# Moving the split maxima, the stores and the gates to other steps of a hand-placed schedule (transformer block on one core)

## The chip, the cores and the metric

The kernel runs on one core of a Trainium2 chip (trn2). The metric is the device time of one execution in microseconds (us), the median of several. Of the kernel before there are three timed executions and one profiled one.

The engines are named as in the profile: PE is TensorE (matmuls; PEld is its weight load), DVE is VectorE, ACT is ScalarE, POOL is GpSimd, SPq is the queue of SyncE, which here issues every DMA. Each engine works through its own instructions in the order in which they are written. It waits only on semaphores.

## What is computed

One transformer block with adaptive layer norm, on x of 2 x 2048 tokens and 256 channels in float32. Cut to what matters:

```
mod = silu(c) @ wmod                      # shifts, scales, gates of both halves
h = layernorm(x) * (1 + ca) + sa
q, k, v = split(h @ W_qkv.T + b_qkv)      # 16 heads of 16
attn = softmax(where(causal, q @ k.T / 4, -inf))
x = x + ga * ((attn @ v) @ W_out.T + b_out)
h = layernorm(x) * (1 + cb) + sb
def mole(x, W, b, A, Bm, Rw):             # E = 3 experts of rank R = 8
    gates = softmax(x @ Rw)
    return x @ W + b + (1 / R) * sum_e(gates_e * (x @ A_e)) @ Bm_e
x = x + gb * mole(relu(mole(h, W1, ...)), W2, ...)
```

## The kernel before

**Steps.** The attention is cut into 32 *units*: one batch, one block J of 512 queries, one group g of 4 heads (`UNITS`). A unit has 4(J+1) *steps*, one for each tile of 128 keys, and there are 320 steps in all. `FIRST[u]` is the first step of unit u. Before step 0 lie 27 steps of preparation (`BEGIN` = -27), and after step 319 some 50 more, in which the last two blocks of the feed-forward half are done.

**One attention step.** PE makes the logits of two pairs of heads (`logits`, L636, and with a mask on the diagonal L641), ACT takes their exponentials (L845), and PE multiplies those by the values two steps later (L700). The last four steps of a unit are on the diagonal, where the widths shrink from 512 to 128.

**The maxima.** The softmax needs each query's maximum before the logits are exponentiated. So a unit's logits are first made once more in the other orientation: PE makes a *pair* (L663, in the diagonal with L671) into two of three PSUM banks, which are taken in turn (`M_BANKS` = 3), and DVE reduces them (`maximum`, L983). `pair_steps` spreads the pairs of unit u over the steps before that unit, about two a step. When the last is done, DVE takes the maximum over blocks and splits it into a rounded part and a rest (`make_parts`, L996, L999, L1000; these are the *split parts*). PE transposes them in step `FIRST[u] - 3` (`turn_maxima`, L682; I call this the *turn* of unit u), DVE copies the result (`copy_parts`, L1008), SP loads it as two more rows of the query tile (L544). PE's turn waits for `m_parts`, which the last instruction of `make_parts` raises.

**The products of the two linear halves.** A block is 256 tokens, and there are 16 of them. The chain `S_CHAIN` makes q, k and v of a block (`s_...`), and `F_CHAIN` does the output projection and the feed-forward half (`f_...`). Each element is a piece of work and its distance in steps from the piece ahead. `S_START` and `F_START` are the first steps of each block. `place()` lays them out, and a PE product gets a step of its own. What a product leaves in its PSUM bank is read by ACT, DVE or POOL at the head of the next step. The products take banks from the same three as the pairs.

**The order within a step** is written out in the loop of each engine. PE: first logits, the turn if there is one, half of the pairs, second logits, values, the other pairs, products. DVE: what products left, `copy_parts`, the step's maxima, then other pieces (statistics, gates), and `make_parts` last of all. SP: loads of queries and keys, `o_rows`, `load_maxima`, then the pieces.

**Pieces that the change touches.** `s_store` issues twelve DMAs of a block's q and k into DRAM (L567), two steps after `s_v`. `stored(b, c)` tells from which step on a block of queries or keys may be read back. `f_load` issues the loads of a block's attention output and row sums (two each, L588 and L589) and of its x (L596). `f_exp` and `f_exp2` are the exponentials of the gates on ACT, `f_gate` and `f_gate2` are what DVE does to them afterwards (L1101 to L1113: sum, reciprocal, scaling, product with the low-rank values and its split), and `f_zturn`, `f_zturn2` are the PE transposes of the result.

Of the kernel before, what the change touches and what calls it, by code (L numbers as in the profile page):

```python
# [15 lines left out]
NH, HD = 16, 16  # L16
# [45 lines left out]
S_CHAIN = [("s_load", 0), ("s_stat", 1), ("s_xhat", 1), ("s_turn", 1), ("s_qk0", 2), ("s_qk1", 1), ("s_v", 1),  # L62
           ("s_store", 2)]
D_CHAIN = [("d_load", 0), ("d_inv", 2), ("d_store", 1)]
F_CHAIN = [("f_load", 0), ("f_norm", 2), ("f_proj", 3), ("f_stat", 2), ("f_xhat", 1), ("f_turn", 1), ("f_base", 0),
           ("f_route", 2), ("f_exp", 1), ("f_gate", 1), ("f_zturn", 1), ("f_hid0", 1), ("f_hid1", 1), ("f_hid2", 1),
           ("f_hid3", 1), ("f_down0", 2), ("f_down1", 1), ("f_exp2", 1), ("f_gate2", 1), ("f_zturn2", 1),
           ("f_low", 1), ("f_out", 2)]
# [141 lines left out]
def key_loads():  # L210

    at = {s: [] for s in range(BEGIN - 1, END)}
    for kb, (u, c) in enumerate(K_BLOCKS):
        need = min(STEP_OF_PAIR[u, k] for k, pair in enumerate(PAIRS[u]) if pair[0] == c)
        step = max(need - LOAD_LEAD, keys_free(kb))
        b, J, _ = UNITS[u]
        assert WHEN["s_store", 2 * (NJ * b + c) + 1] < step < need, (kb, u, c, step, need)
        at[step].append(kb)
    return at
# [5 lines left out]
def query_loads():  # L225

    at = {s: [] for s in range(BEGIN - 1, END)}
    for u in range(NU):
        need = STEP_OF_PAIR[u, 0]
        step = max(need - LOAD_LEAD, FIRST[u - Q_BUFS + 1] if u >= Q_BUFS else BEGIN)  # L230
        b, J, _ = UNITS[u]
        assert WHEN["s_store", 2 * (NJ * b + J) + 1] < step < need, (u, step, need)
        at[step].append(u)
# [6 lines left out]
def build_program(nc, x, cT, wmod, wqkvT, bqkv, bv, woutT, bout, w1, b1, ar1, bl1, w2, b2, ar2, bl2, out):  # L240
# [5 lines left out]
    with ExitStack() as whole:  # L246
# [264 lines left out]
        with nc.Block() as block:  # L511
            @block.sync
            def _(sp):
# [43 lines left out]

                def s_store(n):
                    b, t0 = batch(n), n * TB % S
                    full, hi = s_buffer(n)  # L560
                    for w, (rows, lows) in enumerate(((q_rows, (0, 0, 1)), (k_rows, (0, 1, 0)))):
                        sp.wait_ge(qk_done, 2 * n + w + 1)
                        for slot, low in enumerate(lows):
                            for c in range(KC):
                                m = KC * w + c
                                src = full[:, m] if low else hi[:, m].bitcast(F32)
                                sp.dma_start(rows[b, 8 * c:8 * c + 8, slot * HD:(slot + 1) * HD, t0:t0 + TB],  # L567
                                             src).then_inc(qk_stored[min(n, EARLY)], 16)

# [7 lines left out]
                def d_store(c):  # L577
                    sp.wait_ge(d_done, c + 1)
                    sp.dma_start(r_rows[c].rearrange("h (k x) -> (h k) x", k=P // NH), den[:]).then_inc(d_stored, 16)

                def f_load(n):
                    c, cols = n // 2, slice(n % 2 * TB, n % 2 * TB + TB)
                    sp.wait_ge(d_stored, 16 * (c + 1))
# [3 lines left out]
                    for k in range(KC):  # L587
                        sp.dma_start(fo[:, k, :], o_rows[c, 8 * k:8 * k + 8, 0:HD, cols]).then_inc(fo_in, 16)  # L588
                        sp.dma_start(fd[:, k, :], r_rows[c, 8 * k:8 * k + 8, cols].unsqueeze(1)  # L589
                                     .broadcast_to((8, HD, TB))).then_inc(fo_in, 16)  # L590
                    if n == 0:
# [10 lines left out]
                pieces = {"s_load": s_load, "s_store": s_store, "d_load": d_load, "d_store": d_store,  # L602
                          "f_load": f_load, "f_out": f_out}
                sp.wait_ge(tables, 13)
# [355 lines left out]
            def _(dve):  # L960
# [185 lines left out]
                for s in range(BEGIN, END):  # L1146
# [151 lines left out]
```

## Time and profile before

| | before |
|---|---|
| timed executions | 1594.4, 1594.85, 1597.65 us |
| median | 1594.85 us |
| profiled execution | 1604.27 us, of which the span shown is 1602.5 us |
| PE busy | 1344.8 us, 84% of the span |
| DVE, ACT, POOL busy | 918.7, 790.3, 386.8 us |
| mean granted clock of PE | 0.843 of full speed |

A row of the waits names who waited, for whom, the sum in us, the number of times and the longest. A row of the timeline has the start and the duration in us, the engine, the line, the operation, what it writes and reads, and in brackets the idle time of the engine just ahead of it and what ended that. A row of the windows has a stretch, its length, the busy time of each engine with the number of instructions, the granted clock of PE (1.00 is 2.4 GHz, 0.50 is 1.2 GHz), the share of time in which the DMA engines were busy, and GB/s.

### The profile page before, as it was taken

What the parts mean: (1) busy time and instruction counts of PE and PEld (TensorE: products, weight loads), DVE (VectorE), ACT (ScalarE), POOL (GpSimd) and SP (SyncE); (2) the same over time, 40 slices, a digit from 0 to 9 for tenths busy, and PEclk for the clock granted to TensorE, in tenths of its full rate; (3) what the DMA queues carried; (4) which work ended last, traced back from release to release, by engine and by line L of the source; (5) the groups of instructions that cost most, each with busy time, mean ns of one, the idle gap of its engine ahead of it and who ended that gap; (6) DMA issues with size and microseconds to landing.
All of it is one profiled execution on the core that took longest, in us unless ns stands there. A gap on an engine that the chain in (4) does not pass through costs nothing. (4 is left out here: it accounts for less than half of the span.)

```text
span 1602.5 us, 26356 instructions
## 1 busy us (share of the span) xinstructions
PE 1344.8 (84%) x10096; PEld 770.6 (48%) x10096; DVE 918.7 (57%) x1886; ACT 790.3 (49%) x1193; POOL 386.8 (24%) x534
## 2 busy tenths in 40 slices
PE   4576787998898898889899998988999999999656
PEld 3553443454553555345444454545455465455246
DVE  6353576667666474745644656676667656662023
ACT  2423364566655454654345545555545555465421
POOL 4310112133223211221202122324233231321041
PEclk8758598899997896988859767999899797799857
DMA  5414142225312112231101332132212121100100
GB/s 160 137 56 120 47 121 77 62 57 165 97 51 63 48 28 67 86 103 40 51 21 55 102 97 73 35 103 67 84 58 58 33 61 48 43 17 15 35 20 14
DMA packets 85943, 107.22 MB, mean 67 GB/s; under 512 B 11306, under 2 KB 59378, under 8 KB 85820
## 3 DMA queue, kind: packets, MB, share of 16 engines
q1 hardware_dynamic: 85820, 105.54, 23.0%
q8 instruction: 82, 1.34, 0.4%
q14 instruction: 41, 0.34, 0.1%
HBM read 66.97 MB, written 38.01 MB: 66 GB/s over the span
## 5 line engine op out<-in xcount | busy, mean ns | idle before, releaser
L983 DVE TENSOR_REDUCE mx<-ps 128x1 f32<-128x512 f32 (+3 forms) x1152 | 707.6, 656 | 405.9 <-PE ps L663 211.2
L845 ACT ACTIVATE prob<-ps 128x1024 f32<-128x1024 f32 (+3 forms) x640 | 552.5, 902 | 419.9 <-PE ps L641 217.2
L663 PE MATMUL ps<-kst,qst 48*128 48x512 f32 (+3 forms) x1280 | 322.7, 500 | 120.1 <-DVE mx L983 91.6
L700 PE MATMUL ps<-prob,vw 128*17 128x512 f32 (+3 forms) x2560 | 341.0, 609 | 0.0
L663 PEld LDWEIGHTS ps<-kst,qst 48*128 48x128 f32 x1280 | 144.8, 212 | 401.8 <-issue 293.0
L636 PE MATMUL ps<-qst,kst 50*128 50x512 f32 (+3 forms) x1280 | 295.8, 456 | 7.7 <-ACT prob L845 6.8
L636 PEld LDWEIGHTS ps<-qst,kst 50*128 50x128 f32 x1280 | 138.5, 208 | 70.0 <-ACT prob L845 29.5
L509 POOL TENSOR_TENSOR hid_lo<-hidf,hid_hi 128x512 fp32r<-128x512 f32 x56 | 71.8, 1282 | 276.0 <-ACT hid_hi L934 276.0
L933 ACT ACTIVATE hidf<-ps 128x512 f32<-128x512 f32 x64 | 38.3, 598 | 112.1 <-PE ps L785 108.1
L671 PE MATMUL ps<-mask_q,pick 64*128 64x128 bf16 x1024 | 86.0, 250 | 0.0
L700 PEld LDWEIGHTS ps<-prob,vw 128*17 128x17 f32 x2560 | 43.9, 98 | 86.9 <-issue 54.9
L709 PE MATMUL ps<-fhT_hi,w_hi 128*128 128x256 f32 x256 | 83.9, 328 | 1.1 <-ACT zgT L922 0.9
L641 PE MATMUL ps<-mask_k,pick 64*128 64x128 bf16 x1024 | 83.0, 242 | 0.0
L794 PE MATMUL ps<-w_hi,hid_hi 128*128 128x284 f32 x256 | 73.2, 312 | 5.0 <-DVE hid_lo L509 4.4
L709 PE MATMUL ps<-fhT_lo,w_hi 128*128 128x256 f32 x256 | 76.8, 300 | 0.0
L709 PE MATMUL ps<-fhT_hi,w_lo 128*128 128x256 f32 x256 | 76.5, 299 | 0.0
L1201 POOL TENSOR_TENSOR sf<-sf,s_hi 128x512 f32<-128x512 f32 x28 | 36.9, 1318 | 149.5 <-ACT s_hi L898 149.5
L794 PE MATMUL ps<-w_lo,hid_hi 128*128 128x284 f32 x256 | 70.0, 300 | 0.0
L1121 DVE COPY fz<-ps 128x28 f32<-128x28 f32 x32 | 6.0, 188 | 103.7 <-PE ps L794 103.7
L709 PEld LDWEIGHTS ps<-fhT_hi,w_hi 128*128 128x128 f32 x256 | 53.5, 209 | 23.5 <-issue 12.0
L1243 POOL TENSOR_TENSOR fx<-fx,yg 128x256 f32<-128x256 f32 x32 | 23.5, 734 | 153.7 <-DVE yg L1122 153.7
L794 PEld LDWEIGHTS ps<-w_hi,hid_hi 128*128 128x128 f32 x256 | 50.1, 196 | 14.5 <-issue 9.1
(157 smaller groups left out, 1741.4 us busy)
## 6 DMA issues: line engine op xcount, KB each, us to landing
kst<-k_rows SPq DMA_DIRECT2D x160, 192.0 KB, 3.9
qst<-q_rows SPq DMA_DIRECT2D x64, 192.0 KB, 3.8
o_rows<-o_sb SPq DMA_DIRECT2D x32, 256.0 KB, 2.1
q_rows<-s_hi SPq DMA_DIRECT2D x56, 128.0 KB
k_rows<-s_hi SPq DMA_DIRECT2D x56, 128.0 KB
sx<-in_x SPq DMA_DIRECT2D x16, 256.0 KB, 5.4
fo<-o_rows SPq DMA_DIRECT2D x32, 128.0 KB
fd<-r_rows SPq DMA_DIRECT2D x32, 128.0 KB
```

Source lines behind the costliest of these rows:

```text
L509: eng.tensor_tensor(parts[1], src, parts[0].bitcast(F32), ALU.subtract).then_inc(ready, 1)
L636: last = pe.matmul(ps[:, banks[a], 0:width], kst[half, slot, p, t % 4 * P:(t % 4 + 1) * P], qst[half, u % Q_BUFS, p, skip:BLK], start=True ...
L641: last = pe.matmul(ps[:, banks[a], 0:P], pick[half, w - a + 1], mask_k[half, w - a + 1], start=False, stop=(w == 1))
L663: last = pe.matmul(ps[:, M_BANK + banks[a], at:at + width], qst[half, u % Q_BUFS, p, i * P:(i + 1) * P], kst[half, K_SLOT[u, c], p, 0:widt ...
L671: last = pe.matmul(ps[:, M_BANK + banks[a], at + width - P:at + width], pick[half, w - a + 1], mask_q[half, w - a + 1], start=False, stop= ...
L700: last = pe.matmul(ps[32 * h:32 * h + HD + 1, O_BANK, skip:BLK], vw[:, (NJ * b + t // 4) % V_BUFS, t % 4, g * GH + h, :], prob[:, s % P_BU ...
L709: last = pe.matmul(out, lhs(i, k), rhs(j, k), start=(k == 0 and n == 0), stop=(stop and k == chunks - 1 and n == len(PASSES) - 1))
L794: last = pe.matmul(ps[:, bank, 0:D + ZP], hid[i][:, m, t * P:(t + 1) * P], w2_p[j][:, m, :], start=(e == 0), stop=(e == len(DOWN) - 1))
L845: act.activation(prob[:, s % P_BUFS, 2 * p:2 * p + 2, 0:width], ps[:, bank:bank + 2, 0:width], ACT.Exp).then_inc(a_free, 1)
L933: act.activation(hidf[:].rearrange("p m t -> p (m t)"), ps[:, bank, :], ACT.Relu)
L983: dve.tensor_reduce(mx[:, u % 2, a, both, i, c], ps[:, M_BANK + bank, 0:n * width].rearrange("p (h x) -> p h x", h=n), AX, ALU.max).then_i ...
L1201: pool.tensor_tensor(full[:, half], full[:, half], hi[:, half].bitcast(F32), ALU.subtract).then_inc(qk_done, 1)
```

## The change

Three things are done to the tables and the loops, and no arithmetic is changed.

1. `make_parts(u)` is called in step `PARTS_STEP[u]`: `FIRST[u] - 4` for the first eight units, as before, and `FIRST[u] - 5` for the other 24. The pairs of a unit must be done by then, so that those of units from the ninth on have a last step one earlier. The turn stays in step `FIRST[u] - 3`.
2. `s_store` becomes four pieces of three DMAs each, in the step of `s_v` and the three after it. The last group is thus issued one step later than all twelve were, and `stored` follows it.
3. In the feed-forward chain `f_load` is cut in two: the loads of the second half of the channels and of x form `f_rest`, a step later, and `f_norm` still follows two steps after that. `f_gate` and `f_gate2` come two steps after their exponentials where it was one. A block's chain is so up to three steps longer, and where blocks queue up, later ones start up to three steps later.

```diff
 S_CHAIN = [..., ("s_v", 1),
-           ("s_store", 2)]
+           ("s_store0", 0), ("s_store1", 1), ("s_store2", 1), ("s_store3", 1)]
-F_CHAIN = [("f_load", 0), ("f_norm", 2), ... ("f_exp", 1), ("f_gate", 1), ... ("f_gate2", 1), ...]
+F_CHAIN = [("f_load", 0), ("f_rest", 1), ("f_norm", 2), ... ("f_exp", 1), ("f_gate", 2), ... ("f_gate2", 2), ...]
...
-    return WHEN["s_store", 2 * (NJ * b + c) + 1] + LOAD_LEAD + 1
+    return WHEN["s_store3", 2 * (NJ * b + c) + 1] + LOAD_LEAD + 1
+
+
+PARTS_STEP = [FIRST[u] - MAX_LEAD - (1 if u < 2 * NG else 2) for u in range(NU)]
+PARTS_AT = {s: u for u, s in enumerate(PARTS_STEP)}
...
-            todo.append((max(free), FIRST[u] - MAX_LEAD, u, k))
+            todo.append((max(free), PARTS_STEP[u] + 1, u, k))
...
-                def s_store(n):
+                def s_store(n, m):
...
+                    w, c = divmod(m, KC)
+                    rows, lows = ((q_rows, (0, 0, 1)), (k_rows, (0, 1, 0)))[w]
+                    sp.wait_ge(qk_done, 2 * n + w + 1)
+                    for slot, low in enumerate(lows):
+                        src = full[:, m] if low else hi[:, m].bitcast(F32)
+                        sp.dma_start(rows[...], src).then_inc(qk_stored[min(n, EARLY)], 16)
...
+                def f_heads(n, k):
+                    c, cols = n // 2, slice(n % 2 * TB, n % 2 * TB + TB)
+                    sp.dma_start(fo[:, k, :], o_rows[...]).then_inc(fo_in, 16)
+                    sp.dma_start(fd[:, k, :], r_rows[...]).then_inc(fo_in, 16)
...
+                    f_heads(n, 0)
+
+                def f_rest(n):
+                    f_heads(n, 1)
...
-                    if s + 1 in TURN_AT:
-                        make_parts(TURN_AT[s + 1])
+                    if s in PARTS_AT:
+                        make_parts(PARTS_AT[s])
```

**What moves on DVE around a turn.** The place is the eleventh unit (steps 66 to 71), whose turn is in step 69. DVE before (`mx` are the reductions, `gsum` to `zg` a block's gates, `negm` and `mparts` the split parts, `mT` the copy after the turn):

```order
L1086 TENSOR_TENSOR gexp<-fz,gmax 128x6
L983 TENSOR_REDUCE mx<-ps 128x1 x8
L1101 TENSOR_REDUCE gsum<-gexp 128x2
L1102 RECIPROCAL gsum<-gsum 128x2
L1103 SCALAR_TENSOR_TENSOR gexp<-gexp,gsum 128x6
L1106 TENSOR_TENSOR zf<-fz,gexp 128x48
L1112 CAST zg<-zf 128x2x24 x2
L1113 TENSOR_TENSOR zg<-zf,zg 128x2x24
L996 TENSOR_REDUCE negm<-mx 128x16
L999 CAST mparts<-negm 128x2x8
L1000 TENSOR_TENSOR mparts<-negm,mparts 128x2x8
L1008 CAST mT<-ps 32x128
```

and after (the line numbers are nine higher):

```order
L1095 TENSOR_TENSOR gexp<-fz,gmax 128x6
L992 TENSOR_REDUCE mx<-ps 128x1 x4
L1005 TENSOR_REDUCE negm<-mx 128x16
L1008 CAST mparts<-negm 128x2x8
L1009 TENSOR_TENSOR mparts<-negm,mparts 128x2x8
L992 TENSOR_REDUCE mx<-ps 128x1 x4
L1017 CAST mT<-ps 32x128
L992 TENSOR_REDUCE mx<-ps 128x1 x4
L1110 TENSOR_REDUCE gsum<-gexp 128x2
L1111 RECIPROCAL gsum<-gsum 128x2
L1112 SCALAR_TENSOR_TENSOR gexp<-gexp,gsum 128x6
```

Before, four reductions of the last step and the seven instructions of the gates stood right ahead of the split parts. Now the parts stand four reductions ahead of the turn's copy, and the gates come behind that copy.

**What moves on SP around a block's stores.** The place is block 11 (steps 133 to 136); behind the stores comes the load of the queries of the nineteenth unit. SP before:

```order
L550 DMA o_rows<-o_sb 128x512
L527 DMA kst<-k_rows 48x2x512 x2
L567 DMA q_rows<-s_hi 8x16x256 x4
L567 DMA q_rows<-sf 8x16x256 x2
L567 DMA k_rows<-s_hi 8x16x256 x2
L567 DMA k_rows<-sf 8x16x256 x2
L567 DMA k_rows<-s_hi 8x16x256 x2
L537 DMA qst<-q_rows 48x2x512 x2
```

and after:

```order
L554 DMA o_rows<-o_sb 128x512
L570 DMA q_rows<-s_hi 8x16x256 x2
L570 DMA q_rows<-sf 8x16x256
L531 DMA kst<-k_rows 48x2x512 x2
L570 DMA k_rows<-s_hi 8x16x256
L570 DMA k_rows<-sf 8x16x256
L570 DMA k_rows<-s_hi 8x16x256
L541 DMA qst<-q_rows 48x2x512 x2
L570 DMA k_rows<-s_hi 8x16x256
L570 DMA k_rows<-sf 8x16x256
L570 DMA k_rows<-s_hi 8x16x256
```

The first group of three now stands ahead of `o_rows`, and the last group comes behind the load of the queries, so that three store DMAs stand right ahead of that load where there were twelve.

## Rows read from the trace of the kernel before

**Rows 1.** The page's busy time of each engine, share of the span, instructions.

```profile
PE 1344.8 (84%) x10096; PEld 770.6 (48%) x10096; DVE 918.7 (57%) x1886; ACT 790.3 (49%) x1193; POOL 386.8 (24%) x534
```

**Rows 2.** PE's waits over the whole span: who waited for whom, us, times, longest.

```profile
PE ps L682 <- DVE mparts L1000: 38.9, 21, 5.3
```

**Rows 3.** PE's waits from 300 to 1520 us, turns of units 9 to 32.

```profile
PE ps L663 <- DVE mx L983: 61.9, 120, 1.4
PE ps L682 <- DVE mparts L1000: 29.9, 16, 5.3
...
PE ps L663 <- DMA qst<-q_rows: 2.8, 1, 2.8
```

**Rows 4.** Timeline of PE around the turn of the eleventh unit.

```profile
410.49 0.27 PE L682 MATMUL ps<-ident,mparts 128*32 128x128 f32 x1 [2.84 <-DVE mparts L1000]
```

**Rows 5.** Timeline of DVE in the same stretch.

```profile
407.17 1.29 DVE L983 TENSOR_REDUCE mx<-ps 128x1 f32<-128x512 f32 x2 [0.52 <-PE ps L663]
...
408.75 0.17 DVE L1103 SCALAR_TENSOR_TENSOR gexp<-gexp,gsum 128x6 f32<-128x6 f32 x1
...
410.17 0.18 DVE L1000 TENSOR_TENSOR mparts<-negm,mparts 128x16 fp32r<-128x16 f32 x1
410.80 0.28 DVE L1008 CAST mT<-ps 32x128 fp32r<-32x128 f32 x1 [0.45 <-PE ps L682]
411.23 1.29 DVE L983 TENSOR_REDUCE mx<-ps 128x1 f32<-128x512 f32 x2 [0.15 <-PE ps L663]
```

**Rows 6.** Windows, ACT's L845: the half-clock stretches that begin at a turn's wait.

```profile
612.60:643.40 30.80, 8.73 (x11) 0.50 0.26 72
...
786.70:834.50 47.80, 14.86 (x17) 0.50 0.13 37
...
1117.80:1131.50 13.70, 2.72 (x4) 0.50 0.12 30
...
sum 181.00, ACT 45.45; mean ACT 4.13
```

**Rows 7.** Windows (PE, PEld, DVE, ACT, POOL): steps 174, 154, 107 and 263.

```profile
872.38:877.39 5.01, 3.27 (x33) 1.58 (x30) 4.52 (x10) 3.25 (x6) 2.15 (x8) 1.00 0.57 167
787.93:796.30 8.37, 7.02 (x61) 3.99 (x58) 3.07 (x6) 3.00 (x6) 3.43 (x9) 0.50 0.28 81
584.39:588.57 4.18, 4.18 (x32) 2.53 (x31) 2.58 (x4) 2.92 (x4) 1.29 (x1) 1.00 0.00 0
1276.79:1284.74 7.95, 7.80 (x32) 4.32 (x31) 3.84 (x7) 2.75 (x4) 0.55 (x1) 0.50 0.11 37
```

**Rows 8.** Timeline of PE in steps 174 and 175, four and two pairs.

```profile
874.73 1.05 PE L700 MATMUL ps<-prob,vw 128*17 128x512 f32 x8
...
877.08 0.50 PE L663 MATMUL ps<-kst,qst 48*128 48x512 f32 x2 [0.87 <-DVE mx L983]
...
879.14 1.48 PE L700 MATMUL ps<-prob,vw 128*17 128x384 f32 x8
```

**Rows 9.** Windows of all engines: one half-clock stretch in steps 175 and 176.

```profile
878.90:882.30 3.40, 3.40 (x21) 1.20 (x17) 2.21 (x4) 0.38 (x1) 0.00 (x0) 0.50 0.38 123
```

**Rows 10.** Timeline of SP around the stores of block 11.

```profile
702.19 2.51 SPq L567 DMA_DIRECT2D q_rows<-s_hi  x4
...
710.42 1.36 SPq L537 DMA_DIRECT2D qst<-q_rows  x2
```

**Rows 11.** Timeline of all engines within the wait of the 27th unit's turn.

```profile
1116.97 1.23 DVE L1103 SCALAR_TENSOR_TENSOR gexp<-gexp,gsum 128x6 f32<-128x6 f32 x1
...
1118.25 1.31 POOL L1211 TENSOR_TENSOR fx<-fx,boutg 128x512 f32<-128x512 f32 x1
```

**Rows 12.** Timeline of all engines before step 0: the first pair of maxima.

```profile
74.00 0.43 SPq L556 DMA_DIRECT2D sx<-in_x  x1
...
76.31 0.33 PE L663 MATMUL ps<-kst,qst 48*128 48x128 f32 x2 [2.86 <-issue]
```

**Rows 13.** Groups by line, whole span: busy us and mean ns of one.

```profile
L1103 DVE SCALAR_TENSOR_TENSOR gexp<-gexp,gsum 128x6 f32<-128x6 f32 x32 | 7.3, 227 | 1.1
```

More of the change, by code:

```diff
@@ L62 @@
 S_CHAIN = [("s_load", 0), ("s_stat", 1), ("s_xhat", 1), ("s_turn", 1), ("s_qk0", 2), ("s_qk1", 1), ("s_v", 1),
-           ("s_store", 2)]
+           ("s_store0", 0), ("s_store1", 1), ("s_store2", 1), ("s_store3", 1)]
 D_CHAIN = [("d_load", 0), ("d_inv", 2), ("d_store", 1)]
-F_CHAIN = [("f_load", 0), ("f_norm", 2), ("f_proj", 3), ("f_stat", 2), ("f_xhat", 1), ("f_turn", 1), ("f_base", 0),
-           ("f_route", 2), ("f_exp", 1), ("f_gate", 1), ("f_zturn", 1), ("f_hid0", 1), ("f_hid1", 1), ("f_hid2", 1),
-           ("f_hid3", 1), ("f_down0", 2), ("f_down1", 1), ("f_exp2", 1), ("f_gate2", 1), ("f_zturn2", 1),
+F_CHAIN = [("f_load", 0), ("f_rest", 1), ("f_norm", 2), ("f_proj", 3), ("f_stat", 2), ("f_xhat", 1), ("f_turn", 1), ("f_base", 0),
+           ("f_route", 2), ("f_exp", 1), ("f_gate", 2), ("f_zturn", 1), ("f_hid0", 1), ("f_hid1", 1), ("f_hid2", 1),
+           ("f_hid3", 1), ("f_down0", 2), ("f_down1", 1), ("f_exp2", 1), ("f_gate2", 2), ("f_zturn2", 1),
            ("f_low", 1), ("f_out", 2)]
@@ L216, in key_loads @@
         b, J, _ = UNITS[u]
-        assert WHEN["s_store", 2 * (NJ * b + c) + 1] < step < need, (kb, u, c, step, need)
+        assert WHEN["s_store3", 2 * (NJ * b + c) + 1] < step < need, (kb, u, c, step, need)
         at[step].append(kb)
@@ L231, in query_loads @@
         b, J, _ = UNITS[u]
-        assert WHEN["s_store", 2 * (NJ * b + J) + 1] < step < need, (u, step, need)
+        assert WHEN["s_store3", 2 * (NJ * b + J) + 1] < step < need, (u, step, need)
         at[step].append(u)
@@ L556, in s_load @@
                         sp.dma_start(sx[:, n % 2], x_in[n]).then_inc(sx_in[n % 2], 16)
-                def s_store(n):
+                def s_store(n, m):
                     b, t0 = batch(n), n * TB % S
                     full, hi = s_buffer(n)
[L561 to L568, printed above, removed]
+                    w, c = divmod(m, KC)
[3 more added lines that the diff above has]
+                        src = full[:, m] if low else hi[:, m].bitcast(F32)
+                        sp.dma_start(rows[b, 8 * c:8 * c + 8, slot * HD:(slot + 1) * HD, t0:t0 + TB],
+                                     src).then_inc(qk_stored[min(n, EARLY)], 16)
                 def d_load(c):
@@ L579, in d_store @@
                     sp.dma_start(r_rows[c].rearrange("h (k x) -> (h k) x", k=P // NH), den[:]).then_inc(d_stored, 16)
+                def f_heads(n, k):
+                    c, cols = n // 2, slice(n % 2 * TB, n % 2 * TB + TB)
+                    sp.dma_start(fo[:, k, :], o_rows[c, 8 * k:8 * k + 8, 0:HD, cols]).then_inc(fo_in, 16)
+                    sp.dma_start(fd[:, k, :], r_rows[c, 8 * k:8 * k + 8, cols].unsqueeze(1)
+                                 .broadcast_to((8, HD, TB))).then_inc(fo_in, 16)
                 def f_load(n):
-                    c, cols = n // 2, slice(n % 2 * TB, n % 2 * TB + TB)
-                    sp.wait_ge(d_stored, 16 * (c + 1))
+                    sp.wait_ge(d_stored, 16 * (n // 2 + 1))
                     if n:
@@ L586, in f_load @@
                         sp.wait_ge(x1_done, n)
[L587 to L590, printed above, removed]
+                    f_heads(n, 0)
+                def f_rest(n):
+                    f_heads(n, 1)
                     if n == 0:
@@ L600, in f_out @@
                     sp.dma_start(out_rows[n], fx[:, n % FX_BUFS]).then_inc(y_stored[n % FX_BUFS], 16)
-                pieces = {"s_load": s_load, "s_store": s_store, "d_load": d_load, "d_store": d_store,
-                          "f_load": f_load, "f_out": f_out}
+                pieces = {"s_load": s_load, "s_store0": lambda n: s_store(n, 0), "s_store1": lambda n: s_store(n, 1),
+                          "s_store2": lambda n: s_store(n, 2), "s_store3": lambda n: s_store(n, 3),
+                          "d_load": d_load, "d_store": d_store, "f_load": f_load, "f_rest": f_rest, "f_out": f_out}
                 sp.wait_ge(tables, 13)
```

## The prediction

> **What bounds the kernel now.** I read the page's busy times first. PE is busy for 84% of the span and DVE for 57% [rows 1], so PE sets the time, and what can be won is PE's idle time and the slowness of its half clock. Next come PE's waits. One stands out because it is long each time: the turn (L682) waits for the split parts 21 times, 38.9 us in all and up to 5.3 us at once [rows 2]. Of this 29.9 us in 16 waits falls to the turns of units 9 to 32 [rows 3], and the remaining 9.0 us in 5 waits to the first eight units. The other large wait, for maxima of pairs, is 61.9 us in 120 pieces of half a microsecond [rows 3].
>
> Then I looked at one turn closely. PE stood for 2.84 us until 410.49, so from 407.65 on [rows 4]. DVE was not idle meanwhile: until 408.46 it reduced the pair of step 68, then it did the seven gate instructions, then the split parts until 410.35 [rows 5]. PE waits because three things stand in DVE's order ahead of the one it needs.
>
> Last, the clock. Eleven stretches at the half level (0.50, 1.2 GHz) begin at such a wait of a turn (in one of them during it), among units 9 to 32. They sum to 181.0 us [rows 6].
>
> **What the half clock costs.** I compare steps with the same work. A step on the diagonal with four pairs took 5.01 us at 1.00 and 8.37 us at 0.50, and a step with two pairs and a hidden-layer product 4.18 and 7.95 us [rows 7]. So 40% and 47% of the slow time would be saved. I take 41%, near the first, since most of the 181 us is in steps with little product work. All of it would be worth 181.0 x 0.41 = 74 us.
>
> **The change part by part.**
>
> *Split parts one step earlier (24 units).* The same three instructions are issued, so DVE's work stays as it is (L1000, the last of them, 0.18 us [rows 5]). In the eleventh unit they now stand four reductions, about 2.6 us (two take 1.29 us [rows 5]), ahead of where they stood, and the gates are behind them. With three banks PE can't be further ahead of DVE than the last three takes, so at the turn the parts are made. I expect the wait itself to go at nearly all 24 turns. What is late next: the maxima. PE's second pair of step 69 needs a bank that DVE frees only after its backlog. The lower bound is what DVE itself loses at a turn now: it idles 0.45 us for the turn and 0.15 us for the next pair [rows 5], so 16 x 0.6 = 9.6 us, if DVE is what limits these steps. The upper bound is all 29.9 us. I take 20 us, nearer to the upper end, because in the eleventh unit a PE product (q, k) follows right after the turn, in which DVE catches up, and over the span DVE is idle for 43% [rows 1].
>
> *The clock behind it.* Bounds are 0 and 74 us. The two longest stretches, 30.8 and 47.8 us [rows 6], run on through steps with four pairs at once, in which PE waits 0.87 us again and again, and there the clock fell also without a wait at the turn [rows 8, 9]. I count a third of their 78.6 us as won and half of the other 102.4 us, since every freed turn leaves short waits for maxima that may bring the clock down by themselves: 26 + 51 = 77 us, times 0.41 = 32 us.
>
> *Pairs due one step earlier.* Their number stays. The plan has 14 steps with four pairs where it had 13, and eight with three where it had none; 73 steps, not 65, have none. A step with four pairs holds two waits of 0.87 us [rows 8]; 1.7 us for the new one and a half of one such wait for each of the eight, 3.5 us, make a loss of 5 us. Bounds: 0, if products cover them, and 10.
>
> *Stores in four groups.* Twelve DMAs as before, about 0.6 us of SP each (four took 2.51 us [rows 10]). SP is waited for by PE once between 300 and 1520 us, for the nineteenth unit's queries: 2.8 us [rows 3]. That load was issued at 710.42 right behind twelve stores that had begun at 702.19 [rows 10]. Now three stores stand between it and the key loads, and the last three come behind it, so it is issued as soon as its buffer is free, about 1 us earlier. Gain 1 us, bounds 0 and 2.8. Queued behind the new waits of SP for q and k (from the step of `s_v` on) are key loads, which lead their use by three steps in both plans, and `load_maxima`, with three steps too. That cover hides them. If it were gone, a transfer issued 2 us late would cost PE 2 us once a block, 16 x 2 = 32 us. Nothing in the trace shows it near.
>
> *Gates and `f_rest` a step later.* Same instructions, and the PE transposes behind them move along; I cost it at nothing, covered by the attention steps between. Without cover see the third rival. *Before step 0:* PE waited 2.86 us for its first pair with the v product of block 2 right behind it [rows 12]. That product is now ahead and fills the wait, but the load of block 3's x (74.00 [rows 12]) comes behind six stores, 6 x 0.6 = 3.6 us, and two loads later. Gain up to 2.9, loss up to 3.6; I take 0. *At the end* the last two blocks go through all queues in the same order as before: 0.
>
> Sum: 20 + 32 + 1 - 5 = 48 us. The profiled execution took 1604.27 us, 0.6% above the median of 1594.85; I take the gain off the median: **1547 us**.
>
> **The rivals.**
>
> *First: DVE limits the diagonal steps.* The wait leaves L682 and comes back at L663 <- mx. In its favour: through the 2.84 us DVE was busy [rows 4, 5], and a step with two pairs needs 2.6 us of reductions on DVE, about what PE's own work takes without a product. Against: the backlog at a turn is mostly gates and parts, not reductions. Then 10 us of waits is won and a quarter of the clock's 74, 18 us: 1594.85 - 10 - 18 + 4 = 1571 us.
>
> *Second: the clock falls anyway.* The clock fell at 878.9 after three short waits for maxima with no long wait near [rows 8, 9]: eight matmuls of the values took 1.48 us, at a smaller width than eight that took 1.05. If that is what brings it down, nothing of the 74 us is won, the waits give the lower bound of 9.6, and the pairs lose their 5: 1590 us. The Trainium skill says as much (TensorE: Matmul & The Clock Gate, "A second HAM failure mode: psum-queue depth-cycling"): a kernel that cycles through PSUM banks with tiny idles between groups of matmuls makes the clock swing to and fro. By that rule alone no share of the 74 us would be won. The trace agrees at 878.9, while the two longest half-clock stretches began at a turn's wait.
>
> *Third, slower: gates collide with POOL in front of maxima.* In the 27th unit's turn the gate instruction L1103 took 1.23 us beside a POOL operation of about the same length, where it took 0.17 us elsewhere [rows 5, 11]. That turn's wait is the longest of all, 5.3 us [rows 2], some 2.5 us above the 2.84 of a turn whose gates were not stretched [rows 4], and a half-clock stretch of 13.7 us began in it [rows 6]: 2.5 + 13.7 x 0.41 = 8.1 us for one collision. The mean of L1103 is 227 ns [rows 13], so (227 - 170) / 1060 = 5% of 32, two, are hit now. The chain's shift moves all gates relative to POOL's steps. Before, the turn waited for such gates; now the step's next pair does. Seven more collisions, 57 us, turn the 48 us won into 9 lost: 1604 us. It decides from six on. The Trainium skill's page SBUF — State Buffer ("SBUF: two separate sides") names a mechanism: VectorE with two SBUF inputs or in a two-port mode and GpSimd take a shared port pair by an exclusive lock, and the later one waits for the whole instruction. By it each of the seven gate instructions could wait for one POOL operation, an estimate of 7 x 1.3 = 9 us where the rows show 2.5, and four collisions would decide. The trace agrees on one instruction, 1.23 us instead of 0.17.
>
> *Fourth: it doesn't do what it says.* If DVE is more than a step behind at a turn, the wait stays where it is, and with the clock also: 1592 to 1600 us. The three banks speak against it.
>
> *Fifth: everything is won*, 29.9 + 74 - 4 = 100 us: 1495 us, and anything below 1512.
>
> **How the numbers follow.** Forecast (1512 to 1565) 0.45; first rival 0.22; second 0.10; third 0.14; fourth 0.03; fifth 0.06. A measurement of this kernel can tell about 0.2%, 3 us, from no change. Faster by more than that (below 1591.7): 0.45 + 0.22 + 0.06 + half of the second = 0.78. Within it: the other half and the fourth, 0.08. Slower: 0.14. The range from 1512 to 1597 leaves out the fifth and the third, 0.20.
>
> **What would show it.** In the profile after, the row L682 <- mparts should be below 12 us, with the first eight units' 9 us left. L663 <- mx may grow by up to 15 us over its whole. The mean clock should rise from 0.843 to 0.86 or more (77 us less at half clock is 0.024). DVE's busy time stays within 1% unless gates collide; then the mean of L1103 rises above 300 ns. I am wrong if the L682 row falls and the span doesn't: then either L663 has taken it over (first rival) or the clock stays at 0.84 (second).

## The result and the profile after

| | before | after |
|---|---|---|
| median | 1594.85 us (3 runs, 1594.4 to 1597.65) | 1577.67 us (3 runs, 1573.32 to 1580.21) |
| ratio | 1 | 0.9884, 95% interval 0.9844 to 0.9923 |
| span profiled | 1602.5 us | 1575.9 us |
| PE busy, PE idle in the span | 1344.8, 257.7 us | 1321.8, 254.1 us |
| granted clock | 0.843 | 0.864 |

The change makes the kernel 17 us (1.1%) faster where 48 us were forecast. The direction was right and the size was wrong by almost a factor of three. Three executions a side are few for a spread as wide as this kernel's (below); the same two kernels run again, 12 executions against 29, gave 17 ± 6 us (e4). The executions of one kernel form one continuous spread, so all of them are compared below; the cut at 1.5% above a kernel's fastest, which leaves nine of those 29 and all 12 of e4, would give e4 a ratio of 0.9988 (0.9938 to 1.0039). The two profiled executions differ by more, 26.6 us, because the one of before was a long one for its kernel (1604.27 us against a median of 1594.85).

The profile after has the line of waits that answers to [rows 2], and the one for the maxima that answers to [rows 3] over the whole span. The columns are as before: who waited for whom, us, times, longest.

```profile
PE ps L672 <- DVE mx L992: 121.8, 196, 2.8
...
PE ps L691 <- DVE mparts L1009: 8.8, 5, 2.7
...
PE ps L672 <- DMA qst<-q_rows: 7.7, 2, 4.8
```

The wait for the split parts fell from 38.9 to 8.8 us, by 30.1 us, as forecast: what is left is that of the first eight units. The wait for the maxima stood at 91.6 us over the whole span of before:

```profile
PE ps L663 <- DVE mx L983: 91.6, 166, 1.4
```

It rose to 121.8 us, by 30.2 us. One row took up what the other gave up. That the two match to 0.1 us is chance: in e4, the same kernel profiled again, the rows are 8.5 and 123.6 us. PE's idle time as a whole fell by 3.6 us. What did change is PE's busy time, 1344.8 to 1321.8 us for the same 10096 matmuls. The same instructions took 23 us less, because the clock was higher.

What became of the half-clock stretches can be read from the clock that the two traces record. In the trace after, none of them from the ninth unit's turn on begins within a turn's wait or in the 3 us behind one; before, eleven did, 181 us [rows 6]. But the other stretches of the same part of the kernel sum to some 250 us, where before they summed to some 167. So about 80 us of the 181 came back at other places. Over the whole span the half clock fell from 504 to 430 us.

At the eleventh unit's turn, which answers to [rows 4], the timeline of PE shows the transpose with no idle time ahead of it:

```profile
411.90 0.28 PE L691 MATMUL ps<-ident,mparts 128*32 128x128 f32 x1
```

and DVE had finished the parts 2.2 us before it, ahead of the next unit's reductions, which answers to [rows 5]:

```profile
409.12 0.19 DVE L1005 TENSOR_REDUCE negm<-mx 128x16 f32<-128x48 f32 x1
...
409.56 0.18 DVE L1009 TENSOR_TENSOR mparts<-negm,mparts 128x16 fp32r<-128x16 f32 x1
409.85 1.29 DVE L992 TENSOR_REDUCE mx<-ps 128x1 f32<-128x512 f32 x2
411.65 1.29 DVE L992 TENSOR_REDUCE mx<-ps 128x1 f32<-128x512 f32 x2 [0.51 <-PE ps L672]
```

Where the wait went is seen best at the 27th unit, the longest wait of before (5.3 us). Timeline of POOL, DVE and PE, two steps behind its turn:

```profile
1104.72 1.30 POOL L1220 TENSOR_TENSOR fx<-fx,boutg 128x512 f32<-128x512 f32 x1
1104.92 1.17 DVE L1115 TENSOR_TENSOR zf<-fz,gexp 128x48 f32<-128x48 f32 x1
...
1106.13 1.26 DVE L1121 CAST zg<-zf 128x48 fp32r<-128x48 f32 x2
...
1107.91 1.28 DVE L992 TENSOR_REDUCE mx<-ps 128x1 f32<-128x512 f32 x2
...
1108.73 0.80 PE L672 MATMUL ps<-kst,qst 48*128 48x512 f32 x2 [2.70 <-DVE mx L992]
```

The gates, now in step 230, are stretched by POOL's operations again, and now the pair behind them waits 2.70 us where the turn had waited 5.28.

### The profile page after: what moved, and what is told of

It is laid out like the page before. It is cut to its first block, busy times and chain, and to the rows that moved or that the text cites. A ratio compares the mean times of both kernels' runs of the same rounds, so it can differ in the third digit from the quotient of the medians.

```text
span 1575.9 us, 26356 instructions
## 1 busy us (share of the span) xinstructions
PE 1321.8 (84%) x10096; PEld 758.7 (48%) x10096; DVE 915.0 (58%) x1886; ACT 791.0 (50%) x1193; POOL 387.0 (25%) x534
## 4 chain that ended last, share of the span: by engine, by line
PE 63%; DVE 14%; issue 5%; ACT 4%; POOL 1%; DMA 1%; SPq 1%; POOLq 0%; DVEq 0%; ACTq 0%
PE ps L709 16%; PE ps L672 14%; PE ps L718 14%; DVE mx L992 9%; PE ps L645 8%; PE ps L803 7%; PE ps L680 2%; ACT prob L854 1%; PE ps L650 1%; PE ps L794 1%; ACT sf L907 0%; PE ps L731 0%; DVE f_stats L1022 0%; DVE zg L1121 0%; ACT s_hi L907 0%
## 5 line engine op out<-in xcount | busy, mean ns | idle before, releaser
L672 PE MATMUL ps<-kst,qst 48*128 48x512 f32 (+3 forms) x1280 | 317.4, 492 | 146.6 <-DVE mx L992 121.8
L672 PEld LDWEIGHTS ps<-kst,qst 48*128 48x128 f32 x1280 | 142.7, 208 | 426.2 <-issue 307.7
L709 PE MATMUL ps<-prob,vw 128*17 128x512 f32 (+3 forms) x2560 | 334.4, 598 | 0.0
L709 PEld LDWEIGHTS ps<-prob,vw 128*17 128x17 f32 x2560 | 43.8, 98 | 86.2 <-issue 56.3
L718 PEld LDWEIGHTS ps<-fhT_hi,w_hi 128*128 128x128 f32 x256 | 51.4, 201 | 22.8 <-issue 13.1
```

The lines of the kernel that those rows point to most:

```text
L672: last = pe.matmul(ps[:, M_BANK + banks[a], at:at + width], qst[half, u % Q_BUFS, p, i * P:(i + 1) * P], kst[half, K_SLOT[u, c], p, 0:widt ...
L709: last = pe.matmul(ps[32 * h:32 * h + HD + 1, O_BANK, skip:BLK], vw[:, (NJ * b + t // 4) % V_BUFS, t % 4, g * GH + h, :], prob[:, s % P_BU ...
L718: last = pe.matmul(out, lhs(i, k), rhs(j, k), start=(k == 0 and n == 0), stop=(stop and k == chunks - 1 and n == len(PASSES) - 1))
```

## The experiments

Executions of one kernel spread over some 50 us, and the spread follows the time at half clock, so each kernel below is compared by the mean of all its executions with the mean of the kernel before in the same series. There were five series, each on a chip of its own: e1 to e4, e5 to e8, e9 to e12, e13 and e14, e15 to e17. The kernel before ran 11 to 29 times in each; e2, e3, e4, e7, e8, e9 and e14 ran 12 times, the others six times. "Half clock" is the time in which the clock would have to be at 0.50 to give the mean clock of the execution. Over 98 executions of the kernel before (1565 to 1624 us, mean 1594.7) the time is 1443 us plus 0.316 us for each us at half clock, with a correlation of 0.97, and half clock runs from 391 to 565 us. "Rest" is the difference in time less 0.31 times the difference in half clock: what the clock doesn't explain. The intervals are twice the standard error, about 95%; with six executions they should be up to a fifth wider. Since a kernel's executions differ mostly by the clock, the rest is known better than the mean, to some 2 or 3 us; that the price of 0.31 holds from one kernel to another is an assumption.

| run | mean us | against before | half clock, against before | rest |
|---|---|---|---|---|
| e1 parts only | 1571.3 | -24.8 ± 6 | -56 | -7 |
| e2 stores only | 1585.2 | -10.9 ± 10 | -5 | -9 |
| e3 gates only | 1596.4 | +0.3 ± 7 | -15 | +5 |
| e4 the change | 1578.8 | -17.3 ± 6 | -61 | +2 |
| e5 parts, stores | 1561.8 | -30.0 ± 9 | -45 | -16 |
| e6 parts, stores, f_rest | 1570.2 | -21.7 ± 7 | -37 | -10 |
| e7 parts, stores, gates | 1595.0 | +3.2 ± 6 | +27 | -5 |
| e8 stores, f_rest, gates | 1584.8 | -7.1 ± 6 | -22 | 0 |
| e9 earlier pairs only | 1592.4 | +0.3 ± 7 | +4 | -1 |
| e10 before, half reductions | 1496.8 | -95.3 ± 8 | -117 | -59 |
| e11 parts, half reductions | 1467.5 | -124.7 ± 9 | -167 | -73 |
| e12 parts (28 units), stores | 1559.3 | -32.8 ± 11 | -53 | -17 |
| e13 wait filled | 1572.3 | -28.1 ± 10 | -88 | -1 |
| e14 filled behind the wait | 1599.8 | -0.6 ± 6 | -76 | +23 |
| e15 e12 and bursts filled | 1548.4 | -43.8 ± 10 | -157 | +5 |
| e16 e12 and more filled | 1571.7 | -20.5 ± 8 | -149 | +26 |
| e17 stores, wait filled | 1549.8 | -42.4 ± 9 | -114 | -7 |

**The parts of the change.** e1 has `PARTS_STEP`, the pairs' due step and the call:

```diff
-            todo.append((max(free), FIRST[u] - MAX_LEAD, u, k))
+            todo.append((max(free), PARTS_STEP[u] + 1, u, k))
...
-                    if s + 1 in TURN_AT:
-                        make_parts(TURN_AT[s + 1])
+                    if s in PARTS_AT:
+                        make_parts(PARTS_AT[s])
```

> Only the split parts and the pairs' last step are one step earlier (24 units); stores, gates and f_rest are as before. Theory A (DVE takes over: the wait only changes its name, and what is won is clock): L682-type waits for parts fall from 38.9 to about 9 us, waits for maxima rise from 91.6 to about 120, PE's idle time stays within 5 us, mean clock rises, time 10 to 20 us under the kernel before, that is all of the change's 17 us. Theory B (the gain comes from the stores or the gates): the waits swap as in A, but the time stays within 4 us of before. Theory C (my forecast's step): idle time falls by 20 us.

e2 has the four stores alone:

```diff
-           ("s_store", 2)]
+           ("s_store0", 0), ("s_store1", 1), ("s_store2", 1), ("s_store3", 1)]
```

> Only the stores are cut into four groups over four steps (and what may be read back follows, one step later). Theory A: within 3 us of before, since PE waits for SP's loads only 2.8 us between 300 and 1520 us. Theory B: 5 to 15 us faster.

e3 has the gates alone:

```diff
-("f_exp", 1), ("f_gate", 1) ... ("f_gate2", 1)
+("f_exp", 1), ("f_gate", 2) ... ("f_gate2", 2)
```

> Only f_gate and f_gate2 stand two steps behind their exponentials instead of one. Theory A: the shift moves products to other steps and gates away from some turns; by itself within 6 us of before, either sign. Theory B: 5 to 15 us faster, with less waiting for the parts because gates no longer stand in front of them. The kernel before had 16 such waits, 29.9 us, from 300 to 1520 us.

e4 is the change itself, with no edit.

> The change as it is, on the chip of the three above. All theories: 12 to 22 us under the kernel before.

Measured: the parts alone won 25 us, by the means more than the whole change (the intervals overlap): 17 us as clock and 7 as rest. Theory A stands on the waits, though the gain is above its 10 to 20 us. e1's two rows of waits of PE:

```profile
PE ps L667 <- DVE mx L987: 114.4, 184, 2.7
...
PE ps L686 <- DVE mparts L1004: 7.2, 5, 1.8
```

31.7 us less for the parts, 22.8 us more for the maxima, and PE's idle time is 255.6 us where it was 257.7 (span 1565.1 less 1309.5 busy). The forecast's step, 20 us less idle time, is refuted: e1's idle time fell by 2 us and its rest by 7. The two rows together fell by 8.9 us, near the forecast's lower bound of 9.6. The stores won about 11 us, where theory A had them within 3. A single row of PE's timeline is nearly of that size. Before, the fourth unit's first pair waited for its queries, whose load stood behind the twelve stores of block 3:

```profile
136.38 0.47 PE L663 MATMUL ps<-kst,qst 48*128 48x128 f32 x2 [8.83 <-DMA qst<-q_rows]
```

and in e2 it waited 8.0 us less:

```profile
131.44 0.33 PE L663 MATMUL ps<-kst,qst 48*128 48x128 f32 x2 [0.81 <-DMA qst<-q_rows]
```

The gates alone changed nothing that can be measured, though they took some waits off the turns (26.7 us for the parts in e3, where it was 38.9; the maxima went to 103.1).

**Together.** e5 leaves the gates and `f_rest` as before; e6 to e8 each take one thing out of the whole change.

> Split parts and stores as changed; gates and f_rest as before. In the first four runs (means of all executions) the parts alone gave 25 us, the stores alone 11, the gates alone 0, and the whole change 17. Theory A (what is left of the change, f_rest and the gates a step later, costs 12 to 19 us when the others are there): 1560 to 1567 us, so the best so far. Theory B (parts and stores win the same time, which can't be won twice): 1570 to 1580 us.

> The whole change, but f_gate and f_gate2 one step behind their exponentials again; f_rest stays a step later. Theory A1 (the gates' shift costs): under 1570 us. Theory A2 (f_rest costs) and theory B: 1573 to 1583 us, as the whole change.

```diff
-           ("f_route", 2), ("f_exp", 1), ("f_gate", 2), ... ("f_gate2", 2), ...
+           ("f_route", 2), ("f_exp", 1), ("f_gate", 1), ... ("f_gate2", 1), ...
```

> The whole change, but all of f_load's transfers in one step again; gates stay a step later. Theory A2 (f_rest costs): under 1570 us. Theory A1 and theory B: 1573 to 1583 us.

```diff
-F_CHAIN = [("f_load", 0), ("f_rest", 1), ("f_norm", 2), ...
+F_CHAIN = [("f_load", 0), ("f_norm", 2), ...
```

> The whole change, but the split parts and the pairs' last step where they were. The waits for the parts come back: near 30 us in all. If the parts carry the gain: 1588 to 1600 us, with 460 to 490 us at half clock where the whole change has 423. If the stores carry it: under 1585 us.

```diff
-PARTS_STEP = [FIRST[u] - MAX_LEAD - (1 if u < 2 * NG else 2) for u in range(NU)]
+PARTS_STEP = [FIRST[u] - MAX_LEAD - 1 for u in range(NU)]
```

Parts and stores add up: 25 + 11 against 30 ± 9. With the gates and `f_rest` on top the change is at 17, so the third edit gives back some 13 us of what the other two win (e5 against e4; the two intervals touch). Neither half of it does so simply: `f_rest` on top of e5 is 8 us dearer, gates on top of e5 33 us, and both 13. e6 came out at the edge of theory A1 (under 1570 us), and e7, at 1595.0 us, outside all theories. What the whole edit gives back isn't clock: e4's half clock is lower than e5's against before (-61 and -45 us), but its rest is 18 us higher, and PE idles 260.6 us in e4's profile where it idles 246.4 in e5's. In e7 the clock is against it too: half clock is 27 us above before, in a plan whose work is the same. So where gates and products of the feed-forward half fall can move the clock, and why just that placement is bad I can't say. e8 speaks for the parts but doesn't settle it: without them the gain is 7 ± 6 us where it was 17 ± 6, and the waits for parts are back at 29.6 us, but the time, 1584.8 us, is just inside what I had written for the stores as carriers, and the half clock, 447 us, is below the 460 that I had expected.

**The pairs alone.**

> Only the pairs' last step is one earlier in 24 units; the split parts are still made in the step ahead of the turn, behind that step's maxima (now those of the next unit) and gates. My forecast's loss for the earlier pairs was 5 us. If the order on DVE is what counts, the turns still wait (30 to 40 us in all) and the time is within 6 us of before; if the earlier pairs alone bring the gain, waits for the parts fall to about 9 us and the time by 20 us.

```diff
                     if s + 1 in TURN_AT:
                         make_parts(TURN_AT[s + 1])
```

The due step is changed as in e1, and these lines stay. No difference (+0.3 ± 7, rest -1), and the parts are still waited for, 31.7 us. So it is the place of `make_parts` in DVE's order that brings e1's gain, and the earlier pairs cost nothing that shows, where I had 5 us.

**Is DVE's backlog what takes the wait over?** In e10 and e11 each reduction reads half of its columns, and the exponentials are of a 64th of the logits; both leave out part of the computation.

```diff
-                                          ps[:, M_BANK + bank, 0:n * width].rearrange("p (h x) -> p h x", h=n),
+                                          ps[:, M_BANK + bank, 0:n * width].rearrange("p (h x) -> p h x", h=n)[:, :, 0:width // 2],
...
-                                   ACT.Exp).then_inc(a_free, 1)
+                                   ACT.Exp, scale=0.015625).then_inc(a_free, 1)
```

> The kernel before, with each reduction over the first half of its columns, and the exponentials of a 64th of the logits, so that they stay finite. DVE's reductions fall from 707 to some 400 us. If DVE is what stands behind both kinds of waits, waits for maxima fall from 91.6 to under 40 us and those for the parts from 38.9 to 20 to 30 us, since gates and parts are still in front of the turn.

> The same with the split parts and the pairs one step earlier, and nothing else changed. Theory A (with full reductions the wait only changes its name, because DVE is behind): here DVE isn't behind, so waits for the parts fall by 15 us or more against the run before and waits for maxima don't rise by as much; PE's idle time falls by 10 us or more. If the idle time stays the same here too, the backlog of reductions isn't the reason.

PE's waits in e10, and then in e11:

```profile
PE ps L663 <- DVE mx L983: 48.3, 100, 3.8
PE ps L682 <- DVE mparts L1000: 27.2, 20, 4.6
```

```profile
PE ps L667 <- DVE mx L987: 55.5, 117, 2.6
...
PE ps L686 <- DVE mparts L1004: 5.9, 5, 1.9
```

Here 21.3 us go and 7.2 come back, a third, where with full reductions (before against e1) 31.7 went and 22.8 came back. So DVE's reductions are a large part of what takes the wait over. In e10 itself the waits for maxima fell to 48.3 us, where I had expected less than 40. From e10 to e11 the idle time fell by 5.6 us only (212.7 to 207.1), not the 10 that I had set as the mark, so I count this as a lean towards theory A and no proof. Another part of the wait for the maxima comes with the clock: in e13 below nothing is moved, the clock is higher, and that row rises as well, from 91.6 to 100.9 us. Of the 29 us between e10 and e11, 16 are clock by the 0.31.

**The first units too.** e12 is e5 with the early parts from the fifth unit on.

> Split parts and stores as changed, gates and f_rest as before (the best so far, 1561.8 us mean), and the parts one step earlier in all but the first four units too. Waits for the parts fall from about 8 us to under 2. By theory A these 6 us come back as waits for maxima, and the time is that of the best run within 6 us: 1556 to 1568. By the forecast's step 6 us are won.

```diff
-PARTS_STEP = [FIRST[u] - MAX_LEAD - (1 if u < 2 * NG else 2) for u in range(NU)]
+PARTS_STEP = [FIRST[u] - MAX_LEAD - (1 if u < 4 else 2) for u in range(NU)]
```

The wait for parts fell to 0.9 us, and the time to 1559.3, 2.5 us from e5 and so the same within the spread. The 7 us did not come back as waits for maxima, as theory A wanted (117.8 us against 117.0 in e5), and they were not won as time either (rest -17 against -16).

**Filling the wait instead of moving it.** This is the run that tells cause from company. e13 is the kernel before, with work put in front of the wait in the 14 turns that waited longest from the ninth unit on:

```diff
+                    if u in (9, 10, 12, 14, 15, 17, 18, 21, 22, 23, 25, 26, 30, 31):
+                        for _ in range(7):
+                            pe.matmul(ps[0:32, M_BANK + bank, :], wqkv_p[0][:, 0, 0:32], wqkv_p[0][:, 0, 0:BLK],
+                                      start=True, stop=True)
                     pe.wait_ge(m_parts, u + 1)
```

> The kernel before with nothing moved; in the 14 turns that waited 1.0 us or more from the ninth unit on, PE does seven extra matmuls (128x512, into the turn's own bank, overwritten by it) ahead of the wait, about 1.5 us at full clock. Over 69 executions of the kernel before, a us at half clock went with 0.32 us of time. Theory F (the idle stretch at the turn is what brings the clock down): the waits for the parts shrink by 10 to 20 us, idle time is replaced by work, half-clock time falls by 30 to 60 us and the time by 10 to 20 us, although no wait is moved. Theory G (the moved schedule happens to hold the clock better, the turn's idling is no cause): half-clock time within 15 us of before, time within 6 us.

In e14 the same lines stand behind the wait.

> The control: the same seven matmuls in the same 14 turns, but behind the wait and ahead of the transpose, so that PE idles as before and then has 1.5 us more work. Theory F: waits as before, half-clock time within 25 us of before, time 5 to 25 us above it (14 x 1.5 = 21 us at most). Theory G: the same as the run with the work ahead of the wait, within 8 us.

e13 won 28 ± 10 us by adding 98 matmuls whose result nobody reads. The group of them, busy time and mean, and the wait for the parts in e13:

```profile
L683 PE MATMUL ps<-wqkv_hi 128*32 128x512 f32 x98 | 25.2, 396 | 0.0
```

```profile
PE ps L686 <- DVE mparts L1004: 14.8, 12, 3.5
```

24 us less of waiting for the parts and 25 us more of work, at no cost (rest -1), and half clock fell by 88 us, worth 27. Wait, half clock and time all fell by more than theory F had said, and theory G is out for e13: work at the turn holds the clock, with no step moved. The control surprised me. Its waits for the parts, in two lines because the filling stands between:

```profile
PE ps L684 <- DVE mparts L1004: 29.3, 14, 5.3
...
PE ps L686 <- DVE mparts L1004: 8.6, 7, 2.0
```

They are as before, 37.9 us in all, yet half clock fell by 76 us too, where I expected 25 at most. The 23 us won that way were paid back by the added work, a rest of +23 us against the 21 that 14 times 1.5 us makes. So theory F is refuted in the form that I gave it, and so is G, by which e14 would have been as fast as e13: it isn't the idle stretch as such. More work on PE next to it holds the clock about as well, and ahead of the wait that work is free. Whether the work has to stand near a turn at all these two runs don't tell, since neither puts it elsewhere; in e15 below, work at other places helps too.

**Filling the short waits.** e15 is e12 with two such matmuls between the waits for a pair's two banks, in steps with four pairs or more; e16 has one in each pair of a product-free step with two or three, 128 of them. It also leaves out those of e15 in steps that hold a product and in the step with ten pairs, which its expectation doesn't say: 72 of e15's 132 stay, and 200 are made in all.

```diff
                     for a in range(2):
                         bank, turn = M_AT["max", u, k, a]
+                        if a == 1:
+                            for _ in range(fill):
+                                pe.matmul(ps[0:32, M_BANK + banks[0], :], wqkv_p[0][:, 0, 0:32],
+                                          wqkv_p[0][:, 0, 0:BLK], start=True, stop=True)
...
+                    fill = 2 if 0 <= s and len(first + second) >= 4 else 0
```

> Split parts (all but the first four units) and stores moved, as in the run with 1559.3 us mean, and in steps with four pairs or more two extra matmuls (128x512, into the pair's first bank, overwritten by the pair) ahead of the wait for the pair's second bank: 0.4 us each time, where PE waits 0.87 us now. Theory F (an idle PE brings the clock down): half-clock time falls by another 20 to 40 us from 419, time 1547 to 1555 us. Theory G: 1557 to 1575 us.

> As the run above, and one extra matmul (0.2 us) in every pair of a step with two or three pairs and no product, 200 or so in all. Theory F: half-clock time falls by 40 to 90 us from 419; each us of it is worth 0.32 us, and 200 x 0.2 us of extra work is partly on the path, 10 to 20 us: 1535 to 1560 us. Theory G: 1565 to 1600 us.

> Nothing of the split parts, pairs, gates or f_rest moved: only the stores in four groups, and the seven extra matmuls ahead of the wait in 14 turns. The stores alone gave 11 us, the fill alone 28. If the two add, 1553 to 1563 us against a mean of 1593.7 of the kernel before, as good as the best run with the parts moved.

e15 and e17 are the fastest complete kernels of the study and can't be told apart: 1548.4 and 1549.8 us in the mean, against 1592.2 of before in their series. Both are below the change by more than the intervals (44 ± 10 and 42 ± 9 us under before, against 17 ± 6). e15's time is as theory F said, but its half clock fell by about 100 us from e12's (-157 against -53), where 20 to 40 were expected. Windows of the whole span (PE, PEld, DVE, ACT, POOL, clock) of the kernel before, the change and e15:

```profile
0.00:1602.50 1602.50, 1344.84 (x10096) 770.64 (x10096) 918.71 (x1886) 790.35 (x1193) 386.80 (x534) 0.84 0.23 67
```

```profile
0.00:1575.90 1575.90, 1321.75 (x10096) 758.70 (x10096) 914.98 (x1886) 790.98 (x1193) 386.99 (x534) 0.86 0.24 68
```

```profile
0.00:1547.30 1547.30, 1319.73 (x10228) 749.58 (x10228) 917.99 (x1886) 789.08 (x1193) 386.26 (x534) 0.90 0.25 69
```

e16 has no less half clock than e15 (326 against 318 us) and 26 us of rest: its added work is on the path. Its half clock is that of theory F and its time, 1571.7 us, that of theory G, so it decides nothing between them. e17 moves no parts at all. It fills their wait and cuts the stores, and comes to 1549.8 us, 42 ± 9 under before, where the sum of e2 and e13 is 39; that is 3 us below the range that I had given. Moving the parts and the stores gave 30 and 33 (e5, e12). So nothing shows that the move is worth more than a filled wait.

## Why the prediction was right and wrong

**Right: the wait goes.** I said that L682 <- mparts would be under 12 us with 9 left, and it is 8.8.

The sum was 48 us and the change won 17. By the table, 19 us of that are clock, where I had 32, and the rest is +2, where I had 16 us won outside the clock (20 for the wait, 1 for the stores, 5 lost for the pairs). So 18 of the missing 31 us lie outside the clock and 13 in it.

**Wrong: 20 us of idle time.** This is the step that failed. I took two thirds of the 29.9 us as won because DVE is idle for 43% of the span, and so could catch up. That share is an average over steps of very different kinds. Around a turn the next pair needs a bank within the same step, and DVE was behind by the same reductions and gates. Measured, PE idles 3.6 us less in the profiles, and the rest in the table is +2 us for the change and -7 for the parts alone. My own lower bound, 9.6 us, reckoned from DVE's idle time at a turn, was nearer to what the parts alone gave. The first rival had this step right: the wait came back at L672 <- mx, with 30.2 us for 30.1. Its 18 us of clock are close to the 19 measured, too; its 10 us of waits don't show in the change.

**Too dear: the price of the clock.** I took 0.41 us for a us at half clock, from pairs of steps. Over 98 executions it is 0.32 (0.29 to 0.33 in the five series). One of the two comparisons was wrong in itself: steps 174 and 154 don't have the same work. Step 174's window has 33 matmuls and ten DVE operations, step 154's has 61 and six [rows 7], because the pairs of step 154 are on the diagonal, with masks and smaller widths, and those of step 174 are full ones. So its 40% is no price. The other pair of steps has the same 32 matmuls, but PE is busy in nearly all of it (4.18 of 4.18 and 7.80 of 7.95 us), so it stands for the dearest steps and not for the mean. That steps in which ACT or DVE sets the pace lose less is my explanation for the lower average; no run separates them. (A slip without effect: four of the eleven stretches, not one, begin while PE still waits.) **Nearly right: its amount.** I forecast 77 us less at half clock; e4 has 61 in the mean, and the two profiles differ by 74. So the term was 32 us forecast and 61 x 0.31 = 19 us measured, which is all of the change's 17. My reason for the discount, that freed turns may lose the clock elsewhere, was right: about 80 us did come back at other places. The second rival, that nothing of the clock would be won, is refuted. The sentence of the Trainium skill behind it (TensorE: Matmul & The Clock Gate, "A second HAM failure mode: psum-queue depth-cycling") ties swings of the clock to short idle times between groups of matmuls that take PSUM banks in turn. This case agrees that short waits go with it: filling waits for banks in e15 took another 104 us off the half clock (-53 to -157). It doesn't agree that they are all, since work at the long waits of the turns took 88 us off in e13.

**Stores: 1 us forecast, about 11 ± 10 measured alone (rest -9).** I looked for waits for SP's loads only between 300 and 1520 us, found 2.8 us, and did not look at the 8.8 us at 136 us, behind twelve stores. In the change it is 4.8 us, in e2 0.8.

**Earlier pairs: 5 us forecast, 0 ± 7 measured (e9).** **Gates and `f_rest`: 0 forecast.** Alone the gates cost nothing in time (e3; rest +5), but on top of the other two the edit gives back some 13 us, which is about what the stores won beyond my forecast. The mechanism of the third rival was seen at its place, in the 27th unit, where stretched gates made PE wait 2.70 us. It did not become more frequent: the mean of that gate instruction is 222 ns after, against 227 [rows 13], and the seven gate instructions together take 41.7 us in both profiles.

```profile
L1112 DVE SCALAR_TENSOR_TENSOR gexp<-gexp,gsum 128x6 f32<-128x6 f32 x32 | 7.1, 222 | 1.1
```

The Trainium skill's account of the port pair that VectorE and GpSimd share (SBUF — State Buffer, "SBUF: two separate sides"), by which, for a VectorE operation with two SBUF inputs or in a two-port mode, whichever engine starts first keeps it for its whole instruction, agrees with the stretched operations at 1104.92 and 1106.13: each began 0.1 to 0.2 us behind one of POOL's and ended with it. In number it decided nothing here.

**The fourth and fifth rival** are out: the wait did leave the turn, and the gain was far from 100 us.

**Open** stays why products and gates in just the steps of e7 cost 72 us of half clock more than e5, what in DVE's work beyond the reductions keeps the idle time nearly constant, and what about PE's work around a turn holds the clock, since it isn't the length of the wait (e14).

## What to carry to other kernels

Where an engine waits for a neighbour that is behind by a queue of work, taking one item out of that queue moves the wait to the next item: before counting a wait as won, look at the neighbour's idle time within that wait, not at its share over the span. Where PE's clock falls and rises in a kernel, split each measured difference into clock and rest (here 0.32 us per us at half clock), since an edit may win only the one. And if PE must wait, harmless matmuls in front of the wait are a cheap test for what the clock costs, and may be kept: here they won 28 ± 10 us where the whole change won 17 ± 6. Time each such set, since e16's, at other places, lost what e15's had won.

## What the runs showed of the hardware

- The same program took from 1565 to 1624 us over 98 executions on five chips, and 94% of that variance (0.97 squared) goes with the time at half clock, 391 to 565 us.
- Work that nobody needs made the kernel faster: 98 matmuls in front of the waits gave 28 ± 10 us, and 132 in e15, beside e12's moves, another 11 (means 1559.3 and 1548.4, with intervals that overlap), while 200 in e16, partly at other places, gave too much work on the path.
- The same 98 matmuls behind the waits held the clock nearly as well (half clock -76 against -88 us) with PE waiting for the parts as long as before (37.9 us against 38.9), so the length of the waits alone doesn't decide it.
- A small DVE operation of the gates took 1.17 us and a pair of casts 1.26 us beside POOL operations of 1.30 and 1.25 us, where they take 0.21 and 0.28 us otherwise (rows of the eleventh unit's gates at 408.95 and 409.20 in the profile before).
